# First attention of a two-layer kernel: the two heads of a pair as two 64-row tiles of TensorE

## The chip, the cores and the metric

One core of a Trainium2 chip runs the whole kernel in one launch. The metric is the device time in microseconds (us) of that core, from the first to the last instruction of the program and the little that lies around it. TensorE is called PE here, VectorE DVE, ScalarE ACT, GpSimd POOL, and SP is the queue that issues most of the DMAs. PEld is TensorE's loading of the stationary operand.

## The reference, cut to what matters

Two transformer layers over 2 x 1024 tokens of width 128, each an attention and a mixture of experts, with residuals. The change touches the first attention alone: 16 heads of width 8, softmax over 1024 keys.

```python
xn = _layernorm(x, ln_scale, ln_bias)
q = (xn @ wq).reshape(bs, sl, 16, 8).transpose(0, 2, 1, 3)   # k, v alike
scores = jnp.einsum('bhid,bhjd->bhij', q, k)
probs = jax.nn.softmax(scores / jnp.sqrt(jnp.float32(128)), axis=-1)
out = jnp.einsum('bhij,bhjd->bhid', probs, v)
out = out.transpose(0, 2, 1, 3).reshape(bs, sl, -1) + xn
```

The other stages (first mixture of 8 experts, second attention with 8 heads of width 128, second mixture of 16 experts) are the same in both kernels.

## The kernel before, in words

`layer0_project` normalises, projects to q, k and v, splits q and k into three bf16 parts each and sends the parts to DRAM. From there `load_pair` brings the rows of one pair of heads into SBUF (12 DMAs on SP): `q_stack` holds for each of the two heads (x = 0, 1) 48 rows, the products of the parts with one another (3 + 2 + 1 times 8 rows), so 96 rows for both heads, and there are two `k_stack`s, one for each head, in which the rows of the other head are zero. A product over 96 rows so gives the scores of one head. Rows 96 to 99 of `q_stack` take the negated row maxima, as a high and a low bf16 part for each head, and the same rows of `k_stack` hold ones for its own head (POOL writes them, L398). Four such stacks are in turn.

There are 16 pairs (8 of each batch). Each pair goes through two passes:

- The search: 16 tiles, each 128 queries of one head by all 1024 keys. PE makes a tile with two matmuls of 512 columns over 96 rows into one of two `max_bank`s (L504), DVE reduces it to 128 maxima (L414). After the 16 tiles PE turns the maxima (`turn_maxima`, L512), DVE splits them into two bf16 rows (`split`, L422 and L424), and SP writes them into `q_stack` (`subtract`, L367).
- The scores and their use: eight steps k, each for 128 keys. In a step PE makes four products of 512 columns over 100 rows (two heads, two halves of the queries, L537) into two `score_bank`s in turn, ACT takes the exponential of each (L483), and PE multiplies the four results of the step before with the values (`use`, L548: four 32-column tiles of the array side by side, in fp32, each shown as two records). After eight steps ACT copies the sums (`take`, L474), PE turns them (`turn_heads`, L522) and DVE divides (`divide`).

The search runs `MAX_LEAD` = 22 tiles ahead of the scores; a prologue makes those 22 tiles alone, and then each step k carries two search tiles, of the next pair or the one after it. PE's order in a step is fixed: score 0, score 1, `use` of the step before, in k = 2 `turn_heads`, in k = 6 `turn_maxima`, score 2, score 3, and the two search tiles. The waits: score e needs the exponential e - 2 to be done (its bank), `use` needs all four of its step, search tile m needs the reduction of m - 2. Score 0 of a pair waits for the DMA of the maxima (`shift_in`). All of it is a sequence written out by hand with semaphores.

At the start of the attention stage POOL fills `v_tile` (L388, L391), writes the ones of the `k_stack`s (eight instructions, L398) and then adds the residual (L402, L404, L406), while DVE stages the first values (`stage`, L431) and begins the search. In `layer0_project` POOL clears rows 0 to 95 of the `k_stack`s (L199).

Of the kernel before, what the change touches and what calls it, by code (L numbers as in the profile page):

```python
# [14 lines left out]
ALU = mybir.AluOpType  # L15
# [14 lines left out]
SHIFTS = 2 * NST  # L30
# [86 lines left out]
def load_pair(sp, t, pair, stack, loaded):  # L117
# [3 lines left out]
    for x in range(2):  # L121
        head = bass.ds(pair * (2 * HD0) + x * HD0, HD0)
        first = x * NST
        for part in range(3):
# [3 lines left out]
            sp.dma_start(t.k_stack[stack][x][rows, :], k_dram[0:3 - part, head, :]).then_inc(loaded, 16)  # L128
# [5 lines left out]
def layer0_project(nc, t, d):  # L134
    ctx = ExitStack()
    with ctx:
# [23 lines left out]
        consts_in, zeros_set = sem("consts_in"), sem("zeros_set")  # L160
        NW = 8

        with nc.Block() as block:  # L163
# [7 lines left out]
            def _(sp):  # L171
# [10 lines left out]
                sp.wait_ge(zeros_set, 2 * STACKS)  # L182
# [11 lines left out]
            def _(pool):  # L194
                pool.dma_start(t.rope[:, :, :], d["rope"].rearrange("a p s -> p a s")).then_inc(consts_in, 16)

                for stack in t.k_stack:
                    for x in range(2):
                        pool.memset(stack[x][0:SHIFTS, :], 0.0).then_inc(zeros_set, 1)  # L199
                pool.wait_ge(zeros_set, 2 * STACKS)  # L200
# [97 lines left out]
def layer0_attention(nc, t):  # L298
# [9 lines left out]
    with ctx:  # L308
# [13 lines left out]
        inverse = sb("inverse", [P, 2, P // 8])  # L322
        maxima = sb("maxima", [P, 2, TILES])
# [9 lines left out]
        rows_set, residual_step = sem("rows_set"), sem("residual_step")  # L333
        score_ready, prob_ready, used = sem("score_ready"), sem("prob_ready"), sem("used")
        plain_ready, max_ready = sem("plain_ready"), sem("max_ready")
# [24 lines left out]
        with nc.Block() as block:  # L360
            @block.sync
            def _(sp):
                def subtract(stack):

                    for part in range(2):
                        row = SHIFTS + 2 * part
                        sp.dma_start(q_stack[stack][row:row + 2, :], shift[:, part, :]).then_inc(shift_in[stack], 16)  # L367
# [18 lines left out]
            def _(pool):  # L386
# [6 lines left out]
                pool.wait_ge(ones_set, 4)  # L393
                for i in range(STACKS):
                    for x in range(2):
                        own = [t.identity[SHIFTS:P, SHIFTS + 2 * part + x:SHIFTS + 2 * part + x + 1].broadcast_to([P - SHIFTS, S])
                               for part in range(2)]
                        pool.tensor_tensor(k_stack[i][x][SHIFTS:P, :], own[0], own[1], ALU.add).then_inc(rows_set, 1)  # L398

                pool.wait_ge(rows_set, 2 * STACKS)  # L400
# [8 lines left out]
            def _(dve):  # L409
                def search(g, s, away, n):  # L410
# [3 lines left out]
                    dve.reduce_max(maxima[:, (s + away) % 2, n:n + 1], max_bank[n % 2][:, :], AX_X).then_inc(max_ready, 1)  # L414
# [32 lines left out]
                for m in range(MAX_LEAD):  # L447
                    if m == TILES + 2:
                        split(0, 0)
                    search(0, 0, *divmod(m, TILES))  # L450

                def body(g, s):
                    for k in range(TB):
                        if k == TURN_AT and ahead(g, s, 1):
                            split(g, s + 1)
                        for away, n in searched_at(k):
                            if ahead(g, s, away):
                                search(g, s, away, n)
                        if k == 3 and not first(g, s):
# [1231 lines left out]
```

## Time and profile before

| what | value |
|---|---|
| median of 3 runs | 1151.48 us (1148.94 to 1153.11) |
| span of the profiled execution | 1151.0 us |
| first attention, scores and prologue | about 41 to 453 us of the span |
| PE busy over the span | 1039.5 us (90%) |
| DVE, ACT, POOL busy | 726.9, 662.0 and 298.1 us |
| mean granted clock of PE | 0.953 |

For the profiled execution only its span is given; its own device time is not listed beside it. The span lies 0.5 us under the median of the runs, so times are worked out as differences and added to the median. In the views a row of the timeline gives the start, the length, the engine, the line, the operation with its tiles and how many instructions are merged; in square brackets stands the idle time of the engine before it and what ended it.

### The profile page before, as it was taken

Reading aid. Unit: us, or ns where it says so; the run is one execution under the profiler, and the core shown is the slowest. Engines: PE = TensorE matmul, PEld = TensorE weight load, DVE = VectorE, ACT = ScalarE, POOL = GpSimd, SP = SyncE. Lnnn points to the kernel's source line nnn. Section 1 sums busy time; section 2 is a strip of 40 time slices with the busy share of each in tenths; the row PEclk is TensorE's granted clock in tenths of the full one; section 3 lists DMA queues with packets and bytes.
Section 4 is the critical chain, followed back from the end, with each engine's and each line's share of the span. In section 5 each row is a group of like instructions: output and inputs, shape, how many; then the busy total and the mean of one; then the engine's idle time right before and its main releaser. Section 6 shows DMA issues by size and latency. Waiting matters only on the chain. (4 is left out here: it accounts for less than half of the span.)

```text
span 1151.0 us, 17518 instructions
## 1 busy us (share of the span) xinstructions
PE 1039.5 (90%) x5080; PEld 515.4 (45%) x5080; DVE 726.9 (63%) x1227; ACT 662.0 (58%) x1415; POOL 298.1 (26%) x236
## 2 busy tenths in 40 slices
PE   4499999999999995886799999999999999589997
PEld 3023333333333321422356565665656565456665
DVE  5588888888888852434544454545454544668997
ACT  4047777777777775322355545555554544357887
POOL 5640000000000000000341624343342510256675
PEclk9579999999999999688899999999999999889999
DMA  5200000000000000000000000000000000000001
GB/s 173 101 1 16 21 23 16 14 14 21 21 14 14 15 1 17 9 1 14 0 1 11 0 6 9 0 0 6 9 0 0 5 1 1 11 8 17 16 18 44
DMA packets 21227, 19.22 MB, mean 17 GB/s; under 512 B 5301, under 2 KB 15517, under 8 KB 21173
## 3 DMA queue, kind: packets, MB, share of 16 engines
q1 hardware_dynamic: 19844, 14.92, 4.4%
q0 software_dynamic: 528, 2.10, 0.5%
q10 hardware_dynamic: 800, 1.57, 0.4%
q8 instruction: 22, 0.36, 0.1%
q14 instruction: 33, 0.26, 0.1%
HBM read 14.26 MB, written 4.19 MB: 16 GB/s over the span
## 5 line engine op out<-in xcount | busy, mean ns | idle before, releaser
L483 ACT ACTIVATE probs<-score_bank 128x512 f32<-128x512 f32 x512 | 277.7, 595 | 121.2 <-PE score_bank L537 119.8
L414 DVE TENSOR_REDUCE maxima<-max_bank 128x1 f32<-128x1024 f32 x256 | 301.6, 1220 | 57.0 <-PE max_bank L504 55.0
L537 PE MATMUL score_bank<-q_stack,k_stack 100*128 100x512 bf16 x512 | 164.3, 386 | 7.0 <-ACT probs L483 5.0
L1089 ACT ACTIVATE a_probs<-a_scores,a_lowest 128x896 f32<-128x896 f32 (+7 forms) x128 | 94.7, 740 | 129.7 <-DVE a_lowest L1084 129.1
L504 PE MATMUL max_bank<-k_stack,q_stack 96*128 96x512 bf16 x512 | 143.9, 401 | 17.6 <-PEq L163 12.1
L1301 PE MATMUL a_sum<-a_turned,a_v 128*128 128x512 f32 (+3 forms) x384 | 158.5, 500 | 0.7 <-ACT a_headsT L1235 0.6
L1075 PE MATMUL a_scores<-a_kT,a_qT 128*128 128x512 f32 (+3 forms) x384 | 146.4, 500 | 2.7 <-ACT a_probs L1089 2.5
L548 PE MATMUL summed<-probs,v_tile 128*32 128x512 f32 x1024 | 136.4, 605 | 1.0 <-ACT probs L483 1.0
L1084 DVE TENSOR_REDUCE a_lowest<-a_scores 128x1 f32<-128x896 f32 (+7 forms) x128 | 96.2, 756 | 58.3 <-PE a_scores L1078 58.3
L537 PEld LDWEIGHTS score_bank<-q_stack,k_stack 100*128 100x128 bf16 x512 | 44.0, 97 | 157.4 <-ACT probs L483 143.4
L1433 POOL TENSOR_TENSOR m_gated<-m_linear,m_sigm 128x512 f32<-128x512 f32 x64 | 87.6, 1370 | 48.3 <-ACT m_sigm L1528 48.0
L708 POOL MEMSET m_padded<- 128x96 f32 x1 | 0.2, 178 | 383.4 <-POOLq L360 383.4
L1292 PE MATMUL a_turn<-identity,a_probs 128*128 128x128 f32 x576 | 95.5, 275 | 4.4 <-ACT a_probs L1089 3.5
L1180 DVE COPY a_turned<-a_turn 128x512 f32<-128x512 f32 x96 | 57.4, 598 | 63.2 <-PE a_turn L1292 62.9
L1292 PEld LDWEIGHTS a_turn<-identity,a_probs 128*128 128x128 f32 x576 | 71.5, 142 | 54.6 <-issue 47.1
L504 PEld LDWEIGHTS max_bank<-k_stack,q_stack 96*128 96x128 bf16 x512 | 48.6, 99 | 90.3 <-DVE maxima L414 22.5
L1601 PEld LDWEIGHTS m_down<-m_w,m_gated 128*128 128x128 f32 x512 | 67.8, 197 | 45.3 <-issue 41.5
L1156 POOL TENSOR_TENSOR x<-x,a_part 128x512 f32<-128x512 f32 x32 | 40.6, 1269 | 176.8 <-DVE a_part L1192 176.8
L1075 PEld LDWEIGHTS a_scores<-a_kT,a_qT 128*128 128x128 f32 x384 | 64.0, 194 | 39.1 <-issue 35.7
L1601 PE MATMUL m_down<-m_w,m_gated 128*128 128x128 f32 x512 | 71.1, 284 | 11.4 <-ACT m_scaled L1548 9.7
L1137 POOL TENSOR_TENSOR a_crossed<-a_swapped,rope 128x512 f32<-128x512 f32 x44 | 55.9, 1270 | 95.3 <-ACT a_swapped L1056 95.1
L1056 ACT ACTIVATE a_swapped<-a_proj 64x512 f32<-64x512 f32 x86 | 50.8, 591 | 49.6 <-DVE a_straight L1047 47.6
(203 smaller groups left out, 1242.8 us busy)
## 6 DMA issues: line engine op xcount, KB each, us to landing
rope<-in_rope POOLq DMA_DIRECT2D x1, 2048.0 KB, 11.4
m_w<-in_L_ffn_mlp_w SPq DMA_DIRECT2D x32, 64.0 KB, 1.7
q_stack<-q_parts SPq DMA_DIRECT2D x32, 48.0 KB
k_stack<-k_parts SPq DMA_DIRECT2D x32, 48.0 KB
q_stack<-q_parts SPq DMA_DIRECT2D x32, 32.0 KB
k_stack<-k_parts SPq DMA_DIRECT2D x32, 32.0 KB
out<-x SPq DMA_DIRECT2D x4, 256.0 KB, 2.5
q_parts<-l_q_parts SPq DMA_DIRECT2D x1, 768.0 KB, 3.5
```

Source lines behind the costliest of these rows:

```text
L414: dve.reduce_max(maxima[:, (s + away) % 2, n:n + 1], max_bank[n % 2][:, :], AX_X).then_inc(max_ready, 1)
L483: act.activation(probs[:, k % PROB_STEPS, j, :], score_bank[j % 2][:, :], ACT.Exp, scale=SCALE0).then_inc(prob_ready, 1)
L504: last = pe.matmul(max_bank[n % 2][:, half * CH:(half + 1) * CH], q_stack[stack][0:SHIFTS, qt * P:(qt + 1) * P], k_stack[stack][x][0:SHIFT ...
L537: pe.matmul(score_bank[j % 2][:, :], k_stack[s % STACKS][x][rows, k * P:(k + 1) * P], q_stack[s % STACKS][rows, half * CH:(half + 1) * CH] ...
L548: last = pe.matmul(summed[VW * j:VW * (j + 1), :], v_tile[s % 2][:, j // 2, k, :], probs[:, k % PROB_STEPS, j, :], start=(k == 0), stop=(k ...
L1075: pe.matmul(scores[n % 2][:, first:first + cols], qT[:, b, q, tile * P:(tile + 1) * P], kT[:, b, first:first + cols], start=True, stop=fir ...
L1084: dve.tensor_reduce(out=lowest[:, n % 8:n % 8 + 1], in_=scores[n % 2][:, 0:row_width(n)], op=ALU.max, axis=AX_X, negate=True).then_inc(low ...
L1089: act.activation(probs[:, k % 2, c, 0:row_width(n)], scores[n % 2][:, 0:row_width(n)], ACT.Exp, bias=lowest[:, n % 8:n % 8 + 1], accum_out ...
L1292: last_turn = pe.transpose(turn_bank[m % 2][:, c * P:(c + 1) * P], probs[:, k % 2, c, j * P:(j + 1) * P], t.identity[:, :])
L1301: pe.matmul(sum_bank[:, skipped(k, j):CH], v[:, BLOCKS[k][0], j, :], turned[:, m % SLOTS, skipped(k, j):CH], start=(j == 0), stop=(TURNED_ ...
L1433: pool.tensor_tensor(gated[:, n % 4, :], linear[:, n % 4, :], sigm[:, n % 4, :], ALU.mult).then_inc(gated_ready, 1)
L1601: last = pe.matmul(down_bank[n % 2][:, k, :], gated[:, n % 4, k * P:(k + 1) * P], w2[par][:, :], start=True, stop=True)
```

## The change

The two heads of a pair get 64 rows each. Head 0 has rows 0 to 47 and head 1 rows 64 to 111, in `q_stack` and in a single `k_stack`, so no rows of zeros are needed. Rows 48 and 49 (112 and 113) take the maxima, and POOL fills rows 32 to 63 and 96 to 127 of the `k_stack`s with ones in `layer0_project`, before the rows are loaded, so that the eight instructions of L398 are gone. Each product runs over 48 or 50 rows in the array's upper or lower half (`tile_position=(x * ROW, 0)`), and products of the two heads follow one another: scores in the order (half 0: head 0, head 1), (half 1: head 0, head 1), and a search tile is 128 queries of both heads by 512 keys, one head in each bank of `max_bank`. DVE's reduction then gives two maxima per row, one for each head, over half of the keys. A new small instruction, `join`, takes the greater of the two halves for all 16 columns, once for each pair, and `turn_maxima` waits for it. It stands behind the first search tile of step k = 5, and in the prologue behind tile 16.

```diff
-                pool.wait_ge(ones_set, 4)
-                for i in range(STACKS):
-                    for x in range(2):
-                        own = [t.identity[SHIFTS:P, ...].broadcast_to([P - SHIFTS, S]) for part in range(2)]
-                        pool.tensor_tensor(k_stack[i][x][SHIFTS:P, :], own[0], own[1], ALU.add).then_inc(rows_set, 1)
...
-                    dve.reduce_max(maxima[:, (s + away) % 2, n:n + 1], max_bank[n % 2][:, :], AX_X).then_inc(max_ready, 1)
+                    qt, half = divmod(n, 2)
+                    dve.reduce_max(halves[:, (s + away) % 2, half, :].rearrange("p (x t) -> p x t", x=2)[:, :, qt],
+                                   max_bank[n % 2][:, :].rearrange("p (x k) -> p x k", x=2), AX_X).then_inc(max_ready, 1)
+                def join(g, s):
+                    dve.wait_ge(max_ready, g * (4 * TILES) + (s + 1) * TILES)
+                    if not first(g, s):
+                        dve.wait_ge(maxT_ready, g * 4 + s)
+                    dve.tensor_tensor(maxima[:, s % 2, :], halves[:, s % 2, 0, :], halves[:, s % 2, 1, :], ALU.max).then_inc(joined, 1)
...
-                    for half in range(2):
-                        last = pe.matmul(max_bank[n % 2][:, half * CH:(half + 1) * CH], q_stack[stack][0:SHIFTS, qt * P:(qt + 1) * P],
-                                         k_stack[stack][x][0:SHIFTS, half * CH:(half + 1) * CH], start=True, stop=True)
+                    for x in range(2):
+                        rows = slice(x * ROW, x * ROW + NST)
+                        last = pe.matmul(max_bank[n % 2][:, x * CH:(x + 1) * CH], q_stack[stack][rows, qt * P:(qt + 1) * P],
+                                         k_stack[stack][rows, half * CH:(half + 1) * CH], start=True, stop=True,
+                                         tile_position=(x * ROW, 0))
...
-                    pe.wait_ge(max_ready, g * (4 * TILES) + (s + 1) * TILES)
+                    pe.wait_ge(joined, g * 4 + (s + 1))
...
-                    x, half = divmod(j, 2)
-                    rows, e = slice(0, SHIFTS + 4), s * 32 + 4 * k + j
+                    half, x = divmod(j, 2)
+                    rows, e = slice(x * ROW, x * ROW + NST + 2), s * 32 + 4 * k + j
...
-                    pe.matmul(score_bank[j % 2][:, :], k_stack[s % STACKS][x][rows, k * P:(k + 1) * P],
-                              q_stack[s % STACKS][rows, half * CH:(half + 1) * CH], start=True, stop=True).then_inc(score_ready, 1)
+                    pe.matmul(score_bank[j % 2][:, :], k_stack[s % STACKS][rows, k * P:(k + 1) * P],
+                              q_stack[s % STACKS][rows, half * CH:(half + 1) * CH], start=True, stop=True,
+                              tile_position=(x * ROW, 0)).then_inc(score_ready, 1)
```

The DMAs of `load_pair` and `subtract` keep their number and size and go to other rows.

## Rows read from the trace of the kernel before

**Rows 1.** Stretches: length; PE, PEld, DVE, ACT, POOL busy; granted clock; DMA; GB/s.
```profile
46.00:66.00 20.00, 17.73 (x37) 2.35 (x35) 19.90 (x20) 0.00 (x0) 19.84 (x9) 0.50 0.10 31
69.00:72.50 3.50, 3.50 (x9) 1.09 (x8) 2.85 (x3) 2.05 (x4) 1.99 (x1) 0.50 0.00 0
100.00:400.00 300.00, 299.07 (x1678) 94.91 (x1671) 250.27 (x277) 223.97 (x415) 0.00 (x0) 1.00 0.06 17
431.00:446.00 15.00, 12.14 (x68) 2.78 (x64) 0.55 (x2) 10.91 (x21) 0.00 (x0) 1.00 0.00 0
```

**Rows 2.** Timeline of one step k, with search (start, length in us).
```profile
270.94 0.60 PE L537 MATMUL score_bank<-q_stack,k_stack 100*128 100x512 bf16 x2
271.37 1.09 ACT L483 ACTIVATE probs<-score_bank 128x512 f32<-128x512 f32 x2 [0.50 <-PE score_bank L537]
...
272.02 2.36 DVE L414 TENSOR_REDUCE maxima<-max_bank 128x1 f32<-128x1024 f32 x2 [0.53 <-PE max_bank L504]
...
272.25 0.65 PE L537 MATMUL score_bank<-q_stack,k_stack 100*128 100x512 bf16 x2
272.50 0.10 PEld L537 LDWEIGHTS score_bank<-q_stack,k_stack 100*128 100x128 bf16 x1 [0.37 <-ACT probs L483]
...
272.82 1.06 PE L548 MATMUL summed<-probs,v_tile 128*32 128x512 f32 x8
273.82 0.60 PE L537 MATMUL score_bank<-q_stack,k_stack 100*128 100x512 bf16 x2
```

**Rows 3.** Groups by line (busy us, mean ns of one), 100 to 400 us.
```profile
L414 DVE TENSOR_REDUCE maxima<-max_bank 128x1 f32<-128x1024 f32 x201 | 236.8, 1220 | 47.6 <-PE max_bank L504 46.0
L483 ACT ACTIVATE probs<-score_bank 128x512 f32<-128x512 f32 x403 | 218.7, 595 | 74.4 <-PE score_bank L537 73.2
...
L504 PE MATMUL max_bank<-k_stack,q_stack 96*128 96x512 bf16 x403 | 103.6, 378 | 0.0
...
L431 DVE TENSOR_SCALAR v_tile<-values 128x64 f32 x24 | 3.4, 186 | 0.0
```

**Rows 4.** Timeline of one step of the last pair, without search.
```profile
440.86 0.61 PE L537 MATMUL score_bank<-q_stack,k_stack 100*128 100x512 bf16 x2
441.29 2.16 ACT L483 ACTIVATE probs<-score_bank 128x512 f32<-128x512 f32 x4 [0.72 <-PE score_bank L537]
...
443.74 0.11 PEld L537 LDWEIGHTS score_bank<-q_stack,k_stack 100*128 100x128 bf16 x2 [0.84 <-ACT probs L483]
```

**Rows 5.** Timeline, layer0_project: POOL's memsets and its next work, a small DVE operation.
```profile
2.18 7.22 POOL L199 MEMSET k_stack<- 96x1024 bf16 x8
12.15 0.18 DVE L218 TENSOR_TENSOR l_token_of_root<-l_first_inverse 128x16 f32<-128x16 f32 x1
...
21.65 2.27 POOL L205 TENSOR_TENSOR l_q_parts<-l_rest,l_q_parts 128x512 bf16<-128x512 f32 x2 [12.26 <-ACT l_q_parts L260]
```

**Rows 6.** Groups by line, PE, the whole span: a matmul over 24 rows.
```profile
L827 PE MATMUL m_wgt<-m_weightT,m_spread 24*128 24x512 bf16 x8 | 2.7, 382 | 1.0 <-DVE m_weightT L747 1.0
```

**Rows 7.** Timeline of PE in a step k = 6, with turn_maxima.
```profile
255.73 0.28 PE L512 MATMUL turned<-identity,maxima 128*16 128x128 f32 x1
...
255.84 0.60 PE L537 MATMUL score_bank<-q_stack,k_stack 100*128 100x512 bf16 x2
```

**Rows 8.** Timeline of DVE where the attention stage begins.
```profile
42.35 2.00 DVE L431 TENSOR_SCALAR v_tile<-values 128x64 f32<-128x64 f32 x2 [12.23 <-POOL v_tile L391]
44.27 2.35 DVE L414 TENSOR_REDUCE maxima<-max_bank 128x1 f32<-128x1024 f32 x2
```

**Rows 9.** Groups by line, POOL, 40 to 72 us.
```profile
L398 POOL TENSOR_TENSOR k_stack<-identity 32x1024 bf16<-32x1024 f32 x8 | 14.9, 1892 | 0.1
L402 POOL TENSOR_TENSOR normed<-normed,affine 128x2048 f32<-128x2048 f32 x1 | 4.5, 4496 | 0.1
```

**Rows 10.** Timeline of the prologue up to the first score.
```profile
59.66 2.17 PE L504 MATMUL max_bank<-k_stack,q_stack 96*128 96x512 bf16 x4 [0.19 <-DVE maxima L414]
...
69.16 1.06 PE L537 MATMUL score_bank<-q_stack,k_stack 100*128 100x512 bf16 x2
```

More of the change, by code:

```diff
@@ L29 @@
 NST = 6 * HD0
-SHIFTS = 2 * NST
+ROW = 64
 VW = 32
@@ L122, in load_pair @@
         head = bass.ds(pair * (2 * HD0) + x * HD0, HD0)
-        first = x * NST
+        first = x * ROW
         for part in range(3):
@@ L127, in load_pair @@
             sp.dma_start(t.q_stack[stack][rows, :], q_dram[part, head, :].unsqueeze(0).broadcast_to([3 - part, HD0, S])).then_inc(loaded, 16)
-            sp.dma_start(t.k_stack[stack][x][rows, :], k_dram[0:3 - part, head, :]).then_inc(loaded, 16)
+            sp.dma_start(t.k_stack[stack][rows, :], k_dram[0:3 - part, head, :]).then_inc(loaded, 16)
 def layer0_project(nc, t, d):
@@ L198, in _ @@
                     for x in range(2):
[L199 to L200 removed]
+                        pool.memset(stack[x * ROW + ROW // 2:(x + 1) * ROW, :], 1.0).then_inc(ones_set, 1)
+                pool.wait_ge(ones_set, 2 * STACKS)
                 for u in range(2 * NCH):
@@ L322, in layer0_attention @@
         inverse = sb("inverse", [P, 2, P // 8])
+        halves = sb("halves", [P, 2, 2, TILES])
         maxima = sb("maxima", [P, 2, TILES])
@@ L365, in subtract @@
                     for part in range(2):
-                        row = SHIFTS + 2 * part
-                        sp.dma_start(q_stack[stack][row:row + 2, :], shift[:, part, :]).then_inc(shift_in[stack], 16)
+                        sp.dma_start(q_stack[stack][NST + part:ROW + NST + part + 1:ROW, :], shift[:, part, :]).then_inc(shift_in[stack], 16)
                 for pair in range(1, 3):
@@ L450, in _ @@
                     search(0, 0, *divmod(m, TILES))
+                    if m == TILES:
+                        join(0, 0)
                 def body(g, s):
@@ L455, in body @@
                             split(g, s + 1)
-                        for away, n in searched_at(k):
+                        for i, (away, n) in enumerate(searched_at(k)):
                             if ahead(g, s, away):
                                 search(g, s, away, n)
+                            if k == TURN_AT - 1 and i == 0 and ahead(g, s, 1):
+                                join(g, s + 1)
                         if k == 3 and not first(g, s):
@@ L494, in search @@
                     m = (s + away) * TILES + n
-                    x, qt = divmod(n, TB)
+                    qt, half = divmod(n, 2)
                     stack = (s + away) % STACKS
@@ L546, in use @@
                     pe.wait_ge(prob_ready, g * (4 * 32) + (s * 32 + 4 * k + 4))
-                    for j in range(4):
-                        last = pe.matmul(summed[VW * j:VW * (j + 1), :], v_tile[s % 2][:, j // 2, k, :], probs[:, k % PROB_STEPS, j, :],
-                                         start=(k == 0), stop=(k == TB - 1), tile_position=(0, VW * j))
+                    for slot in range(4):
+                        x, half = divmod(slot, 2)
+                        last = pe.matmul(summed[VW * slot:VW * (slot + 1), :], v_tile[s % 2][:, x, k, :], probs[:, k % PROB_STEPS, 2 * half + x, :],
+                                         start=(k == 0), stop=(k == TB - 1), tile_position=(0, VW * slot))
                     last.then_inc(used, 1)
@@ L1634, in two_layers @@
             t.q_stack = [early_sb(f"q_stack{i}", [P, S], BF16) for i in range(STACKS)]
-            t.k_stack = [[early_sb(f"k_stack{i}_{x}", [P, S], BF16) for x in range(2)] for i in range(STACKS)]
+            t.k_stack = [early_sb(f"k_stack{i}", [P, S], BF16) for i in range(STACKS)]
             layer0_project(nc, t, d)
```

15 lines of the change are left out of this document (4 added, 11 removed).

## The prediction, written before the changed kernel ran

> **What bounds the kernel now.** I read the stretches first [rows 1]. In the steady part of the first attention PE is busy 299.07 of 300 us, DVE 250.27 and ACT 223.97, the granted clock is 1.00. That looks like a kernel bound by PE, and the change halves PE's time for eight of the twelve products of a step. But busy time of a matmul includes its fill, so I looked next at single steps.
>
> One step of the timeline, from score 2 to the next score 2 [rows 2]: 270.94 score 2; 271.37 the exponential of it starts (0.43 later). One exponential is 595 ns long [rows 3], the two together 1.09, so that of score 3 starts 0.49 later, at 271.86, and ends at 272.46. At 272.50 PE loads the weights of score 1 of the next step, which waited for ACT just there; its matmul starts at about 272.52 (two from 272.25 take 0.65, one is 378 ns [rows 3]). `use` starts 0.30 later, 272.82, and takes 1.00 to score 2 at 273.82. This is a ring:
>
> 0.43 (score 2 to its exponential) + 0.49 (to the next one) + 0.60 (that one's length) + 0.06 (to score 1) + 0.30 (to `use`) + 1.00 (to score 2) = 2.88 us, which is the whole step, 273.82 - 270.94. It exists because `use` needs all four exponentials, score 1 needs the last one, and score 2 stands behind `use` in PE's order. PE's own work between `use` and score 1 (scores 2 and 3, four search matmuls, score 0) just fits beside the ACT part: the wait for ACT ahead of the last weight load shows that it came last.
>
> Is the ring or PE's load the bound, when both are so near? The last pair answers: its steps have no search. The same step there goes from 440.86 to 443.74, again 2.88 us [rows 4], though four matmuls of some 0.22 (0.60 - 0.38 is the distance of two) are gone, 0.87 us of PE's time. ACT sat idle 0.72 before it, and DVE was busy 0.55 of 15 us in that stretch [rows 1]. So taking PE's search work away altogether saved nothing. The ring sets the step.
>
> **The steady steps, part by part.** The pairs free PE at four places. Scores 0 and 1: score 0 may start as soon as its exponential of the step before is done, but score 1 waits for the last one, 0.49 later; they can't be issued together, and score 1 is the one on the ring. Scores 2 and 3 may run together; exponential 3 starts 0.49 after exponential 2 in any case, more than the 0.22 that score 3 comes earlier. The search tiles (four times 0.22, now perhaps half) lie beside ACT. So of the ring's six terms none contains work that is taken away: 0 us. If the pairs did not overlap at all, PE would have the work of before and the result would be the same.
>
> DVE: the reduction reads the same 1024 columns; I take 1220 ns again [rows 3]. Two in a step take 2.36, with 0.53 idle [rows 2]; the added `join` is a 128x16 operation, 0.18 by the row of one [rows 5], once for each pair, behind the first tile of k = 5. It delays the second reduction, whose tile PE delivers some 0.4 earlier than before. `turn_maxima` waits for `join`, but stands in k = 6 behind `use`, more than a microsecond after it. What a late `join` would hold is the `split`, SP's two DMAs of the maxima and score 0 of the next pair: it would take about 0.5 us more before that reached score 1. Cost 0.
>
> The ring's unknowns: **fill.** A matmul's 0.38 is 0.21 of streaming (512 columns at 2.4 GHz) and 0.17 of fill. Does a 64-row tile fill faster? The nearest rows say no: 24 rows take 382 ns, 96 rows 378 [rows 3, 6], both in the whole array. Bounds: 0, or half of the fill, 0.08, once in the ring (score 2), times 127 steps = -10 us. I take 0. **Switch of the array's form.** From score 1 to `use` is 0.30 where streaming is 0.21, from `use` to score 2 it is 1.00 where the two passes of its tiles stream 0.85 to 0.90; some 0.10 are lost at each change between whole array and 32-column tiles. After the change it is between two 64-row tiles and four 32-column tiles. I take the same 0.10, because that is the nearest row; the bounds are 0.10 and the full fill of 0.17, so up to +0.07 x 2 x 127 = +18 us.
>
> **New switches.** Today `turn_maxima` is followed by score 2 after 0.11 [rows 7], its bare streaming (two passes of 128 columns at 2.4 GHz): both use the whole array. Afterwards the score is in another form. That happens on the ring, behind both kinds of turn: 15 times each. 30 x 0.10 = **+3.0 us** (bounds 0 and 30 x 0.17 = 5).
>
> The Trainium skill, "TensorEngine Tiling (Array Packing)", section Key Properties, says that a change of tiling mode drains TensorE; the same page's section Theoretical Speedup puts dimensions up to 64 at up to 2x. The trace agrees with the first by the 0.10; the second would halve the eight products, of which the ring holds nothing.
>
> **The prologue.** At its start DVE stages the first values with two small instructions. In the loop they take 186 ns each [rows 3]; here the two take 2.00, and the first reduction starts only at 44.27 [rows 8]. POOL's L398 runs just then, 1.892 us long [rows 9]: the second instruction waited for it. The change removes the eight L398, and the next in POOL's order is L402, 4.496 us long [rows 9]. It will start in the same place, at 42.4, and DVE will be held until 46.9: 4.5 - 1.9 = **+2.6 us**. The bounds are -1.8 (nothing holds DVE any more) and +2.6. I take the upper one, since the wait was as long as POOL's whole instruction.
>
> The Trainium skill, "SBUF — State Buffer", section Who interferes with whom, states this as a lock on a shared port for a whole instruction, and the 2.00 agrees. If DVE and POOL only shared the bandwidth, the length of POOL's next instruction would not matter, and the term would be 0 instead of +2.6.
>
> The tiles then run in a ring of their own at the low clock: reduction, search matmuls, next reduction, four matmuls each 2.17 + 0.19 idle = 2.36 for two tiles [rows 10]. With heads side by side PE's part shrinks and DVE's pace of 2.28 (two intervals of 2.36 - 1.22 = 1.14) is the bound: nine pairs of tiles x 0.07 = -0.6. `join` stands in this chain, +0.2. From `split` to score 0 nothing changes. The removed 14.9 us of POOL otherwise shorten only its own list. The start of the scores moves by **+2.2 us**.
>
> **The clock.** In the prologue the clock is 0.50 (1.2 GHz), in spite of PE being busy 17.73 of 20 us [rows 1]; it rose only after 3.5 us without a gap at the first scores [rows 1]. Afterwards the first step has gaps, since score 2 waits for an exponential and not for matmuls. I expect the clock to rise one step later. A step at 1.2 GHz would be 4.15 (the ring with `use` and each stream doubled: 2.88 + 0.85 + 0.21 + 0.21), so +1.3. Less 0.3, since in the first step score 2 comes 0.67 + 0.60 + 0.06 = 1.33 after score 0, by its exponential, and no longer behind four streams of 0.43: **+1.0 us**. That it holds afterwards is shown by the last pair: clock 1.00 through 431 to 446 us with PE busy 12.14 of 15 us [rows 1], and the changed steps leave PE at about the same load.
>
> **Edits at no cost.** The memsets in `layer0_project` are of ones and 32 rows instead of 96, of the same length in the free direction: 7.22 us for eight, then 12.26 idle [rows 5]. The cover would hold even at twice the length. DMAs keep number and size; SP's order is untouched. `take` stays on the ring of k = 0 as it is.
>
> **Sum.** 0 (steady) + 3.0 + 2.2 + 1.0 = +6.2 us on 1151.5: **1157.7 us**. What a measurement of this kernel can tell from no change is about 0.3%, 3.5 us.
>
> **The rivals.**
> - Ring shorter by the fill: -10 + 6 = -4, 1147 us. For it: half the rows to cross. Against: [rows 3, 6]. Chance 0.09, with 0.02 more for half of it, which is no measurable change.
> - PE is the bound after all: then the next limit is DVE, 250.27 us [rows 1] for 201 / 16 = 12.6 pairs [rows 3], 19.9 a pair and with `join` and waits some 20.6, instead of 300 / 12.6 = 23.8; 3.2 x 15 = -48, + 6: about 1110 us. Against it is the step of 2.88 without search. This is the other side in full: it decides if the steps fall below 2.8. Chance 0.05.
> - Dear switches: each costs the full fill. +18 + 2 + 6: 1178 us. A new form may drain more than a known one. Chance 0.11.
> - The low clock stays: the prologue shows 0.50 under a load that is high. Each step then costs 1.27 more, all 127 of them +161: up to 1320 us; a pair or two of them +10 to 20. For: the first line of [rows 1]. Against: at the low clock PE's streams fill over 90% of a step. Chance 0.05.
> - The change doesn't do what it says, the halves run one after the other: the steady steps as forecast, the prologue 0.6 longer, 1158 us. Chance 0.06.
>
> Forecast 0.62, with its own range 1153 to 1163. Faster by over 0.3%: 0.09 + 0.05 = 0.14. Within 0.3% (below 1155.0): 0.20 of the forecast's 0.62 (switches free, or no hold by POOL, or an early clock), 0.02 and 0.02: 0.24. Slower: 0.62. The range for 8 in 10 reaches down towards the shorter ring and up to most of the dear switches: 1148 to 1172.
>
> **What would show it.** In the changed trace: score 2 to score 2 still 2.88 us in steps with search, ACT idle about 0.7 once in a step instead of twice, waits for ACT ahead of both score 0 and score 1; PE's search tile 0.22 long instead of 0.43; `turn_maxima` to score 2 about 0.21; DVE's two L431 together 4.6 us and the first reduction near 46.9; first score near 71.4. I am wrong if the steps get shorter than 2.8 (then PE was the bound) or longer than 3.0 (switches), or if the granted clock is under 1.00 behind 80 us.

## The result and the profile after

The changed kernel takes 1168.0 us (1165.3 to 1171.4, 4 runs), the kernel before 1150.4 in the same comparison: a ratio of 1.014, interval 1.011 to 1.017, which is 16 us slower (the medians lie 17.6 apart). The forecast was +6.2 us. The direction and most of the mechanisms were right, the size was not: one term, the clock, was 17 us instead of 1 in the profiled run, which is the longest of the four (1171.4 us).

The stretches of the changed kernel come first, in the columns of [rows 1]: the first steps, the steady part, the part before the search ends, the part after it.

```profile
76.00:90.00 14.00, 14.00 (x60) 2.34 (x54) 7.07 (x6) 6.51 (x12) 0.00 (x0) 0.50 0.00 0
100.00:400.00 300.00, 262.19 (x1663) 62.15 (x1663) 249.29 (x287) 222.77 (x414) 0.00 (x0) 1.00 0.06 18
405.00:432.00 27.00, 23.16 (x148) 5.43 (x144) 20.29 (x24) 19.95 (x37) 0.00 (x0) 1.00 0.01 2
437.00:465.00 28.00, 23.90 (x86) 3.94 (x86) 0.55 (x2) 14.14 (x27) 0.00 (x0) 0.50 0.00 0
```

In the 300 us of the steady part PE has 37 us less to do than before, and DVE and ACT did nearly as much as before (249.29 for 250.27 us, 222.77 for 223.97): the pace is almost unchanged. PE's gain became idle time. The first and the last line show what changed the total: the granted clock is 0.50 at both ends of the attention. In [rows 1] it was 1.00 in the last steps, and before the change it had risen at 73 us.

One steady step of the changed kernel in its timeline, against [rows 2]:

```profile
254.95 0.39 PE L540 MATMUL score_bank<-q_stack,k_stack 50*128 50x512 bf16 x2
...
255.37 2.24 ACT L488 ACTIVATE probs<-score_bank 128x512 f32<-128x512 f32 x4 [0.72 <-PE score_bank L540]
255.60 2.35 DVE L407 TENSOR_REDUCE halves<-max_bank 128x2 f32<-128x1024 f32 x2 [0.52 <-PE max_bank L510]
...
256.02 0.87 PE L540 MATMUL score_bank<-q_stack,k_stack 50*128 50x512 bf16 x2 [0.25 <-ACT probs L488]
256.51 0.09 PEld L540 LDWEIGHTS score_bank<-q_stack,k_stack 50*128 50x128 bf16 x1 [0.40 <-ACT probs L488]
...
256.83 1.07 PE L553 MATMUL summed<-probs,v_tile 128*32 128x512 f32 x8
257.82 0.10 PEld L540 LDWEIGHTS score_bank<-q_stack,k_stack 50*128 50x128 bf16 x2 [0.84 <-ACT probs L488]
```

Two scores side by side take 0.39 together, instead of 0.60, so the tiles do overlap. And the step, from the weight load of score 2 (254.94, with the first row shown) to the next one, is 257.82 - 254.94 = 2.88 us, to the hundredth that of before. Scores 0 and 1 stand half a microsecond apart (0.87 for the two), each behind its own exponential.

The start of the attention stage, the rows that answer to [rows 8] and [rows 9], and the turn of the maxima, to [rows 7]:

```profile
43.08 4.49 POOL L394 TENSOR_TENSOR normed<-normed,affine 128x2048 f32<-128x2048 f32 x1
43.17 4.55 DVE L432 TENSOR_SCALAR v_tile<-values 128x64 f32<-128x64 f32 x2 [12.13 <-POOL v_tile L391]
...
47.64 3.47 DVE L407 TENSOR_REDUCE halves<-max_bank 128x2 f32<-128x1024 f32 x3
...
263.58 0.28 PE L519 MATMUL turned<-identity,maxima 128*16 128x128 f32 x1
...
263.79 0.39 PE L540 MATMUL score_bank<-q_stack,k_stack 50*128 50x512 bf16 x2
```

DVE's two small instructions end with POOL's long one, as forecast (4.55 us, forecast 4.6), and the turn is 0.21 ahead of the score instead of 0.11.

Where the time went can be read from the starts of `use` in both timelines. Before, the same four uses (behind the first step, four steps later, in the k = 6 of the last but one pair, the last one):

```profile
73.19 1.06 PE L548 MATMUL summed<-probs,v_tile 128*32 128x512 f32 x8
...
84.73 1.06 PE L548 MATMUL summed<-probs,v_tile 128*32 128x512 f32 x8
...
421.77 1.06 PE L548 MATMUL summed<-probs,v_tile 128*32 128x512 f32 x8
...
451.08 1.06 PE L548 MATMUL summed<-probs,v_tile 128*32 128x512 f32 x8 [0.96 <-ACT probs L483]
```

After:

```profile
75.03 1.93 PE L553 MATMUL summed<-probs,v_tile 128*32 128x512 f32 x8
...
91.57 1.06 PE L553 MATMUL summed<-probs,v_tile 128*32 128x512 f32 x8
...
430.73 1.06 PE L553 MATMUL summed<-probs,v_tile 128*32 128x512 f32 x8
...
470.86 1.94 PE L553 MATMUL summed<-probs,v_tile 128*32 128x512 f32 x8 [1.17 <-ACT probs L488]
```

The distance grows from 1.84 us to 6.84, 8.96 and 19.78. The first score comes 2.2 later (71.39 instead of 69.16; forecast 2.2). Then 0.4 is gained in the first step (forecast 0.3). Four steps at the low clock give 5.0. The 337 us in between, with 28 of the 30 turns, give 2.1. The last steps, eight of them at the low clock, give 10.8, and the last use and turn after them 1.3 more. The sum is 21.1 us at the end of the attention; the later stages, whose code is the same, gave 2.6 of it back, and the spans differ by 18.5. These stages are no fixed sum: from the start of the last `use` to the end of the span they took 699.9 us before and 697.1 to 703.9 in the profiles of the runs below that leave them and `use` as they are.

### The profile page after: what moved, and what is told of

It is laid out like the page before. It is cut to its first block and busy times, and to the rows that moved or that the text cites. A ratio compares the mean times of both kernels' runs of the same rounds, so it can differ in the third digit from the quotient of the medians.

```text
span 1169.5 us, 17540 instructions
## 1 busy us (share of the span) xinstructions
PE 1005.8 (86%) x5080; PEld 478.9 (41%) x5080; DVE 730.7 (62%) x1243; ACT 661.9 (57%) x1415; POOL 284.1 (24%) x228
## 5 line engine op out<-in xcount | busy, mean ns | idle before, releaser
L407 DVE TENSOR_REDUCE halves<-max_bank 128x2 f32<-128x1024 f32 x256 | 301.9, 1219 | 59.6 <-PE max_bank L510 59.5
L540 PE MATMUL score_bank<-q_stack,k_stack 50*128 50x512 bf16 x512 | 155.9, 409 | 49.6 <-ACT probs L488 37.9
L553 PE MATMUL summed<-probs,v_tile 128*32 128x512 f32 x1024 | 147.7, 651 | 1.2 <-ACT probs L488 1.2
L540 PEld LDWEIGHTS score_bank<-q_stack,k_stack 50*128 50x128 bf16 x512 | 36.3, 93 | 246.7 <-ACT probs L488 221.2
L510 PE MATMUL max_bank<-k_stack,q_stack 48*128 48x512 bf16 x512 | 86.0, 405 | 27.6 <-DVE halves L407 15.5
L1606 PE MATMUL m_down<-m_w,m_gated 128*128 128x128 f32 x512 | 71.4, 284 | 11.5 <-ACT m_scaled L1553 10.3
L1553 ACT ACTIVATE m_scaled<-m_down,m_column 128x128 f32<-128x128 f32 x256 | 72.0, 369 | 0.3 <-PE m_down L1606 0.3
```

What stands on the lines that cost most here:

```text
L407: dve.reduce_max(halves[:, (s + away) % 2, half, :].rearrange("p (x t) -> p x t", x=2)[:, :, qt], max_bank[n % 2][:, :].rearrange("p (x k) ...
L540: pe.matmul(score_bank[j % 2][:, :], k_stack[s % STACKS][rows, k * P:(k + 1) * P], q_stack[s % STACKS][rows, half * CH:(half + 1) * CH], s ...
L553: last = pe.matmul(summed[VW * slot:VW * (slot + 1), :], v_tile[s % 2][:, x, k, :], probs[:, k % PROB_STEPS, 2 * half + x, :], start=(k == ...
L1553: last = act.activation(scaled[:, n % 2, k, :], down_bank[n % 2][:, k, :], ACT.Copy, scale=column[n // NCH][:, tile, :])
L1606: last = pe.matmul(down_bank[n % 2][:, k, :], gated[:, n % 4, k * P:(k + 1) * P], w2[par][:, :], start=True, stop=True)
```

## The experiments

They start from the changed kernel, unless the text says that it is the kernel before.

**Extra matmuls in the steps without search.** Where the search has ended, PE makes four matmuls (`TAIL_FILL` = 4) of 48 rows by 512 columns into the free `max_bank`s, which nobody reads.

```diff
                         for tile in tiles:
                             search(g, s, *tile)
+                        if not tiles:
+                            if k == TURN_AT - 1:
+                                pe.wait_ge(max_ready, NPAIR * TILES)
+                            fill(s % STACKS, TAIL_FILL)
```

> The changed kernel, and in the eleven steps without search tiles PE makes four extra matmuls of 512 columns over 48 rows, whose results nobody reads (extra work, the output is unaffected). Theory A (the clock falls because the search ends and the paired products leave PE gaps): the granted clock stays 1.00 to the end of the attention; in the changed kernel's trace the last use started 10.8 us later against the kernel before than the use at 430.7 us did, so the time falls by 10 to 12 us. Rival B (the fall comes from the 64-row form itself, whatever the gaps): the clock still falls near 436 us and the time is the same within 1 us. Rival C (the fall is no cause, steps of 4.18 us come from a dearer switch): no change or slower by four matmuls a step.

Measured 1156.9 us (1.0052, 1.0035 to 1.0068 of before). The clock holds to the end of the attention:

```profile
437.00:458.00 21.00, 20.12 (x122) 5.37 (x114) 0.55 (x2) 14.51 (x27) 0.00 (x0) 1.00 0.00 1
```

From the `use` in the k = 6 of the last but one pair to the last one it is 29.46 us (427.66 to 457.12) instead of 40.13: 10.7 us are the clock in the last steps, and more work on PE takes them away. B and C are out. That leaves open whether idle time or thin work let the clock fall. The 11 us between the medians are not this alone: in this profile the first steps had one low step and not four, though their code is the same.

**Scores not paired.** The old order of the four scores, in which neighbours use the same 64 rows.

```diff
-                    half, x = divmod(j, 2)
+                    x, half = divmod(j, 2)
...
-  probs[:, k % PROB_STEPS, 2 * half + x, :]
+  probs[:, k % PROB_STEPS, 2 * x + half, :]
```

> The changed kernel with the scores in the old order (head 0 half 0, head 0 half 1, head 1 half 0, head 1 half 1), so that scores 0 and 1, and 2 and 3, use the same 64 rows and can't overlap; the search stays paired. Theory A (gaps in time on PE decide the clock): each step has 0.22 us more of streaming, as much in the last steps as the kernel before had there, and before the clock held; so the clock holds through the last pair, at the start it rises some steps earlier, and the time falls by 10 to 15 us. Rival B (the number of rows in use counts, not only the time): 50 rows for as long as 100 before are half the rows, so the clock falls at 436 us again, same time. In both, steady steps stay 2.88 us, since the ring does not hold the overlap.

Measured 1166.7 us (1.0143, 1.0103 to 1.0184): no gain. The clock in the last steps:

```profile
428.00:446.00 18.00, 14.33 (x81) 3.22 (x77) 1.31 (x6) 13.20 (x26) 0.00 (x0) 1.00 0.01 2
449.00:462.00 13.00, 11.73 (x42) 1.47 (x42) 0.00 (x0) 6.03 (x12) 0.00 (x0) 0.50 0.00 0
```

PE now streams in these steps for as long as in the kernel before, where the clock held for all of them ([rows 1]: busy 12.14 of 15, here 14.33 of 18). It held to 447 us instead of 436 and then fell all the same. The later moment says little: with the paired scores and the same last steps it fell at 440 and at 454 us in two of the runs below. But the fall itself, at as much streaming as before, does not fit my theory A, gaps in time, and rows at work became the better one.

**POOL waits for the staged values.** One line, `pool.wait_ge(staged, 2)`, ahead of the residual work.

> The changed kernel, but POOL begins its residual work only when DVE has staged the first values. Theory: the two staging instructions take about 0.3 us instead of 4.55, the first reduction starts 4.3 us earlier and the first score too, so -4.3 us, if the clock rises the same number of steps later. Rival: POOL's work held nothing, the 4.55 has another cause (the first touch of the tile, the loading of values): no change. Third: the residual work now ends later but is finished long before it is read, so it costs nothing either way.

Measured 1157.8 us (1.0050, 1.0034 to 1.0067), 10 us less than the changed kernel instead of 4.3.

```profile
43.38 0.30 DVE L433 TENSOR_SCALAR v_tile<-values 128x64 f32<-128x64 f32 x2 [12.19 <-POOL v_tile L391]
```

The two instructions take 0.30. The first score comes at 67.3 instead of 71.4, the forecast 4; and the clock rose at 75 us, one step after the first use, so that three of the four low first steps were gone too (3.9 us). At the end, where the code is that of the changed kernel, the clock fell at 440 us, and four steps were low instead of eight (5.5 us). Why an earlier start also shortens the time at the low clock I can't tell.

**The same in the kernel before**, where the first of POOL's instructions is shorter (`pool.wait_ge(staged, 2)` in place of the wait ahead of L398).

> The kernel before, and POOL writes the ones of the k_stacks only when DVE has staged the first values. Theory of the shared port: the 2.00 us of the two staging instructions become 0.3, the first reduction comes 1.7 us earlier, so does the first score (POOL's ones are ready long before), and the time is 1.7 us less, 0.15%. Rival: POOL's late ones now hold something (score 0 waits for them): 0 or slower.

Measured 1150.7 us, ratio 0.9978 (0.9960 to 0.9995): 2.5 us less, with 1.7 expected inside the interval. The two instructions took 0.30, the first score came at 67.5.

**Extra matmuls at the first scores**, of 48 rows and of 128 rows:

```diff
                     search(0, 0, *divmod(m, TILES))
+                    warm({TILES + 3: 3, TILES + 4: 2}.get(m, 0))
...
                         if first(g, s) and k == 0:
+                            warm(1)
```

> The changed kernel with six extra matmuls of 512 columns over 48 rows ahead of and in the first step of the scores (three behind search tile 19, two behind tile 20, one between score 1 and the first search tile), results unused. Theory A (PE had gaps in the first steps and in the wait for the maxima, and these keep the clock low): the clock rises near 73 us instead of 91, four steps of 4.18 us become 2.88, -5 us, less up to 0.5 for the matmuls that stand in the way. Rival B (rows count): the extra work is as narrow as the rest, so the clock rises at about the same step, 0 to +0.5 us.

> As the run with six extra matmuls of 48 rows at the first scores (it had 1166.6 us, clock up at 92 us in its profile), but each of the six goes over all 128 rows, results unused. Theory R (rows at work count, which the kernel before with 50-row scores showed over the whole attention): the clock rises near 73 to 76 us and the time is 3 to 6 us less, about 1162. Rival (only time counts): the same number of matmuls of the same length, so again 1166 to 1167.

Measured 1166.6 us (1.0132, 1.0115 to 1.0149) and 1168.7 us (1.0110, 1.0077 to 1.0144). Neither helped: the clock rose at 92 and at 88 us in the profiles, and the first score came 0.8 and 1.2 us later than in the changed kernel. In the wide run single runs went from 1161 to 1171. Six matmuls, wide or narrow, did not decide it, and the forecast of both theories for the wide ones failed.

The wide run's profile shows something else. Its last steps are those of the changed kernel, yet the clock held to 454 us, and two steps were low instead of eight:

```profile
437.00:453.00 16.00, 11.85 (x72) 2.69 (x72) 0.55 (x2) 12.01 (x23) 0.00 (x0) 1.00 0.00 0
```

Its last `use` starts at 463.04, 7.8 us earlier than in the changed kernel, and the span is only 2.6 shorter: the later stages took the rest. So the loss in the last steps is not a fixed 10.8 us for this code. In the four profiles with the same last steps it was 10.8, 10.8, 5.4 and 2.8.

The changed kernel itself has two groups of runs, 1165.3 with a mean clock of 0.943 and 1171 with 0.930. Four low steps more or less would be 4 x 1.3 = 5.2 us, but only a run of the longer group was traced, so it is not shown that this is the difference. The unpaired run, with the same two mean clocks, was traced in its shorter group: there both ends were better, with the clock up at 79 us and down at 447.

**Scores over 50 rows in the kernel before, and over 96 as its control.** The first is a pure test of the rows: no tiles, no pairs, the old order. Both leave out the subtraction of the maxima, the first the second head's rows too.

```diff
-                    rows, e = slice(0, SHIFTS + 4), s * 32 + 4 * k + j
+                    rows, e = slice(0, 50), s * 32 + 4 * k + j        # control: slice(0, SHIFTS)
```

> The kernel before (whole array, one head for each product, nothing paired), but each score product runs over rows 0 to 49 of the stacks instead of 0 to 99: it leaves out the rows of the second head and the subtraction of the maxima. Same instructions, same streaming time, half the rows at work in the scores. Theory R (the rows that are at work count for the granted clock): the clock falls in the last steps as it did in the changed kernel with unpaired scores (447 us there), and the time grows by 5 to 9 us. Theory T (the form of the tiles or the time alone counts): the clock holds to the end of the attention as before, time the same within 2 us.

> Control for the run in which the kernel before had scores over 50 rows (1206 us, low clock to 267 us in its profile): the same kernel with scores over rows 0 to 95. It too leaves out the subtraction of the maxima, so that probabilities are larger, but both heads' rows are at work. Theory R (rows at work count): the clock rises at 73 us and holds, time as before within 3 us. Rival D (the other data, larger probabilities and sums in use, kept the clock low there): a low clock here too and 1190 us or more.

Over 50 rows: 1206 us, ratio 1.041 (1.036 to 1.045). Its profile is of its longest run, 1269 us, with a mean clock of 0.866; the four that the ratio rests on took 1195 to 1207, with 0.919 to 0.933, against 0.950 to 0.954 of the kernel before. Taken as means over time between 0.50 and 1.00, these give an estimate of 50 to 90 us more at the low clock than in the kernel before, and of 230 for the profiled run. So the direction holds for every run, the 150 us below for the longest alone. In the profile the clock stays low until 267 us. Over 96 rows: 1152.5 us, 0.9991 (0.9971 to 1.0011), clock up at 73 us. The stretch from 100 to 250 us, 50 rows and then 96 (in the second fence):

```profile
100.00:250.00 150.00, 150.00 (x433) 25.61 (x432) 65.46 (x72) 57.64 (x107) 0.00 (x0) 0.50 0.03 10
```

```profile
100.00:250.00 150.00, 149.52 (x843) 47.55 (x835) 124.67 (x137) 111.98 (x208) 0.00 (x0) 1.00 0.06 17
```

PE is busy without a gap for 150 us and the clock stays at 1.2 GHz: how long PE is busy does not decide the clock alone. But low it is only until it has once risen. From 268 to 537 us the same products run at the full clock:

```profile
350.00:400.00 50.00, 50.00 (x267) 13.46 (x266) 39.73 (x45) 35.49 (x67) 0.00 (x0) 1.00 0.05 16
```

What bears on the changed kernel's main loss is the end, the eleven steps without search. Over 50 rows, ahead of the fall and behind it:

```profile
531.00:537.00 6.00, 4.67 (x25) 0.90 (x24) 0.37 (x3) 4.87 (x10) 0.00 (x0) 1.00 0.01 3
540.00:560.00 20.00, 18.69 (x60) 3.11 (x56) 0.55 (x2) 9.77 (x18) 0.00 (x0) 0.50 0.00 0
```

Over 96 rows, at about the same steps:

```profile
428.00:434.00 6.00, 4.66 (x28) 0.92 (x24) 0.00 (x0) 4.93 (x10) 0.00 (x0) 1.00 0.00 0
434.00:450.00 16.00, 13.14 (x74) 2.90 (x66) 0.55 (x2) 11.20 (x22) 0.00 (x0) 1.00 0.00 0
```

PE is busy 4.67 and 4.66 of 6 us. With 50 rows the clock then falls and the steps become 4.18 us, as in the changed kernel; with 96 it holds to the end. No tile, pair or order of scores differs between the two, so it is the rows of the score products that let the clock fall. The missing subtraction is in both, so it is not the cause. One difference in the data is not separated: over 50 rows the second head's products keep two of its own rows. The changed kernel and its unpaired version, whose products are whole, lose the clock at the same end.

**Both repairs together.**

> The changed kernel with both repairs: extra matmuls in the eleven steps without search, and POOL's residual work only when DVE has staged the first values. If the two causes are separate they add up: -11 us and -9 us as measured one by one against the changed kernel's 1168, of which the second held some of the start's low clock too; 1150 to 1154 us. If they are one cause seen twice (the later part of the clock's fall moved), 1156.

Measured 1155.9 us (1.0017, 1.0000 to 1.0033). That is the 1156 forecast for one cause seen twice. In the profiles of both runs with one repair three of the four low first steps were already gone, so that part of their gains is the same one. And the later stages took part of the gain: the last `use` starts at 452.32, 4.8 us earlier than with the extra matmuls alone, the span is 1.8 shorter. What is left against the kernel before is 2 us. In the profile the turns cost 2.3 and the one low step 1.1, and 2.3 are gained ahead of them and in the first step.

**The ring opened: `use` in two parts.** The claim under the whole prediction is that the step is a ring of waits through `use`. If so, it must get shorter when only half of `use` stands in it. Both repairs are in these kernels, other than in the kernel before with the same cut.

```diff
-                def use(g, s, k):
+                def use(g, s, k, part):
+                    cols = slice(part * (CH // 2), (part + 1) * (CH // 2))
...
+                        if done:
+                            use(*done, 0)      # behind score 1
...
                         for j in range(2, 4):
                             score(g, s, k, j)
+                        if done:
+                            use(*done, 1)      # behind score 3
                         for tile in tiles:
                             search(g, s, *tile)
```

> The kernel with both repairs, and the use of the probabilities cut into two parts of 256 columns, one behind score 1 and one behind score 3; ACT takes the heads behind the fourth exponential of k = 0. Theory (a ring of waits through use sets the step at 2.88 us): from score 1 to score 2 only half of use remains, about 0.84 us instead of 1.30; then PE's order and DVE (2.28 for two reductions and 0.25 of other work a step) are the limit, a step of 2.5 to 2.6, so 127 x 0.3 = 38 us less, 1112 to 1120 us. Rival (DVE or the banks set the step already): no gain, and slower by two more changes of the array's form in each step, 127 x 0.2 = +25 us.

Measured 1160.6 us (1.0079, 1.0047 to 1.0111), not 1115. Its timeline shows a second ring:

```profile
252.19 0.38 PE L548 MATMUL score_bank<-q_stack,k_stack 50*128 50x512 bf16 x2
...
252.68 2.16 ACT L490 ACTIVATE probs<-score_bank 128x512 f32<-128x512 f32 x4 [0.80 <-PE score_bank L548]
...
253.34 0.87 PE L548 MATMUL score_bank<-q_stack,k_stack 50*128 50x512 bf16 x2 [0.19 <-ACT probs L490]
...
254.14 0.64 PE L562 MATMUL summed<-probs,v_tile 128*32 128x256 f32 x8
...
254.71 0.61 PE L512 MATMUL max_bank<-k_stack,q_stack 48*128 48x512 bf16 x4
...
255.15 0.38 PE L548 MATMUL score_bank<-q_stack,k_stack 50*128 50x512 bf16 x2
```

Scores 0 and 1 now stand together at 252.19; score 3 waits for exponential 1 (253.82), then the second part of `use` (254.14), then the search (254.71), then score 0 again: 2.96 us, of which the search is 0.44.

That is not all of the time. Twice, where PE goes back to the start of its loop over the pairs, it stands idle for about 3 us and waits for nothing that the trace shows, and the clock falls with it (for 10.2 us from 190.6 on, for 6.8 from 289.6 on):

```profile
189.55 0.51 PE L548 MATMUL score_bank<-q_stack,k_stack 50*128 50x512 bf16 x2 [3.00 <-issue]
...
290.76 0.72 PE L548 MATMUL score_bank<-q_stack,k_stack 50*128 50x512 bf16 x2 [2.93 <-issue]
```

No run with `use` in one piece has such a gap there. The cut doubles the matmuls of `use`, and the queue that brings instructions moved twice as much, here and in the three runs below; first without the cut (both repairs), then with it:

```profile
q8 instruction: 22, 0.36, 0.1%
...
q8 instruction: 44, 0.72, 0.2%
```

So the longer loop is probably fetched anew on each pass; no run tests this. Away from the gaps a pair of eight steps mostly takes 23.5 to 23.9 us instead of 24.02 uncut: a step with a turn is no longer than the others. The four pairs at the gaps take 26.8, 27.1, 26.9 and 24.9. These 11 us turn a gain of 5 into a loss.

**The kernel before with the same cut.**

> The kernel before, whole array, with the same cut of use. Theory: the ring is opened here too, but now PE's own work is the limit: 12 streams of 0.22, 0.87 of them search, use 0.85, four changes of form at 0.1, together about 3.0 us, so the step gets no shorter than 2.9 to 3.05 and the time is 1150 to 1172 us. If the gain of the cut is as large here as in the kernel with two 64-row tiles, the pairing has no part in it.

Measured 1204.5 us (1.0448, 1.0425 to 1.0471), outside of what I expected. The step is 3.40 us:

```profile
249.97 0.64 PE L549 MATMUL summed<-probs,v_tile 128*32 128x256 f32 x8
...
253.37 0.64 PE L549 MATMUL summed<-probs,v_tile 128*32 128x256 f32 x8
```

That is the second ring with the search of before in it: 2.96 - 0.44 + 0.87 = 3.39. My sum of PE's work missed it. The two gaps are here too (2.36 and 2.50 us), with 3.4 us of low clock behind each. The pairing matters here as it never did in the closed ring: the search costs half.

**The search between score 1 and score 2**, and then **one search tile in each ring**:

> The run with use cut in two had steps of 2.96 us: score 0 to its exponential 0.49, this and the next 0.49 + 0.60, score 3 0.07 later, 0.32 to the second part of use, 0.57, and then the search 0.44 ahead of the next score 0: a new ring through the search. Here the search tiles stand behind the first part of use, where PE waited for an exponential. Theory: the ring loses the 0.44, steps of 2.5 to 2.6 us, with DVE nearly as long; 127 x 0.35 = 44 us less than the 1160 of that run, about 1115, less what a low clock gives back. Rival (something else holds the steps, DVE's reductions or ACT): no shorter than 2.9.

Measured 1173.2 us (1.0161, 1.0139 to 1.0183), worse than the first cut, although the step is no longer. In its profile the clock rose at 91.6 us instead of 74.6, which costs 6 us in the first pair, a pair takes 24.1 us, since the turns stand in the ring again, and the two gaps and the low clock behind them cost 11. The first parts of `use`:

```profile
256.48 0.64 PE L562 MATMUL summed<-probs,v_tile 128*32 128x256 f32 x8
257.05 0.61 PE L512 MATMUL max_bank<-k_stack,q_stack 48*128 48x512 bf16 x4
...
259.36 0.64 PE L562 MATMUL summed<-probs,v_tile 128*32 128x256 f32 x8
```

2.88 us again: the search's 0.44 moved into the first ring (last exponential, score 1, first part of `use`, score 2), which without it would be 2.45. The two together tell what each ring can bear.

> Two rings were measured with use cut in two: last exponential, score 1, first part of use, score 2, exponentials 2 and 3: 2.89 us with the search's 0.44 in it (2.45 without); and score 0, exponentials 0 and 1, score 3, second part of use, score 0: 2.96 with the 0.44 in it (2.52 without). Here one search tile stands in each, 0.22: 2.67 and 2.74, so the step is 2.74 us, 127 x 0.22 = 28 us less than the 1160.6 of the first of the two, 1133, and 15 more or less by the clock. Rival (the rows of these two runs misread, another limit near 2.9): 1155 to 1175.

```profile
265.27 0.64 PE L562 MATMUL summed<-probs,v_tile 128*32 128x256 f32 x8
265.84 0.39 PE L512 MATMUL max_bank<-k_stack,q_stack 48*128 48x512 bf16 x2
...
266.53 0.64 PE L562 MATMUL summed<-probs,v_tile 128*32 128x256 f32 x8
267.10 0.39 PE L512 MATMUL max_bank<-k_stack,q_stack 48*128 48x512 bf16 x2
...
267.94 0.64 PE L562 MATMUL summed<-probs,v_tile 128*32 128x256 f32 x8
```

The step shown is 267.94 - 265.27 = 2.67 us; a pair with its turns takes 22.2 to 22.7, 2.8 a step. The time is 1140.1 us, ratio 0.9887 (0.9862 to 0.9912): the first version that beats the kernel before, by 13 us. The expected 1133 was too low by 7. The gaps account for that: PE is idle for 2.63 and 2.67 us at the loop's return, the clock falls for 3 us near 184 and for 10 near 276, and the four pairs there take 9 us more than the others.

```profile
275.66 0.72 PE L548 MATMUL score_bank<-q_stack,k_stack 50*128 50x512 bf16 x2 [2.67 <-issue]
```

## Why the prediction was right and wrong

- **The ring sets the step, 0 us from the pairs.** Right. The step stayed 2.88 us although PE lost 37 of 300 us of busy time, and the ring gave way only when `use` was cut: a pair of eight steps went from 24.02 us to 22.2 to 22.7 with one search tile in each ring.
- **Fill and switches.** Right in kind: score 2 to its exponential is 0.43 as before, `use` to score 2 1.00. The new switch behind a turn is 0.10. The 337 us between the outer uses hold 28 of the 30 turns and grew by 2.1 us where 2.8 were forecast for them, 0.08 each.
- **The prologue, +2.2.** Right to the tenth at the first score; within it the hold by POOL was 2.55 (forecast 2.6), the tiles' pace and `join` gave back 1.14 (forecast 0.4), and the stage itself began 0.82 later, for which I have no cause.
- **The clock, +1.0. This is the step that failed.** In the profiled run it measured 5.0 us in the first steps, 10.8 in the last ones and 1.3 behind them, 17.1, less the 0.4 gained in the first step: 16.7. The price of a low step was right, 4.18 us for a forecast 4.15 (79.21 - 75.03, by the starts of `use` there). The expectation that the clock rises one step later failed by three steps. What failed above all was the sentence that the last pair shows that the clock holds, since "the changed steps leave PE at about the same load". Load was read as busy time, and even that was less: PE is busy 11.85 of 16 us in such steps at the full clock (in the run with wide extra matmuls), and was 12.14 of 15. And the row had scores over 100 rows; the changed ones go over 50. Unpaired scores brought the busy time back, and the clock still fell; over 50 rows it fell and over 96 it held, with nothing else changed in the kernel before. As a rival ("The low clock stays") I had it at 0.05, "a pair or two" of low steps at +10 to 20, and for a reason in time only. The size of the term is partly luck of the run: in the four profiles with these last steps the loss there was 2.8 to 10.8 us.
- **The rival of the dear switches** would have given 1178 us and is not what happened, although its time is near: the switches cost 0.08 to 0.10.
- **Open.** What sets the moment at which the clock rises in the first steps: with the same code there it was 91 us in the profile of the changed kernel and 79 in that of the run with extra matmuls at the end, and extra matmuls ahead of it did nothing. What sets the moment of the fall: 436, 437, 440 and 454 us with the same last steps. Why the later stages, with the same code, took 697 to 704 us. Why PE stands idle at the loop's return with `use` cut.

## What to carry to other kernels

When the busiest engine is relieved, look first for a stretch of the same trace in which its work is already missing: here the last pair's steps, as long without search as with it, showed that PE's load did not set the pace. A relieved TensorE may also lose its clock, and busy time alone does not tell: here scores over half of the rows lost it where those over nearly all of them, at the same busy time, did not. So compare the rows at work too. The room that such a change makes is worth something only when the ring of waits is opened for it, and where the freed work then stands decides which ring it lengthens. A cut that doubles the instructions in a loop has a price of its own: look for gaps at the loop's return.

## What the runs showed of the hardware that was not expected

- PE busy for 150 of 150 us, with scores over 50 rows beside products over 96 and 128, at a granted clock of 0.50 (in the longest run of that kernel); with scores over 96 rows and the same instructions the clock was 1.00. Once risen, it was 1.00 with 50 rows too, for 270 us, until the search ended.
- PE idle for 2.4 to 3.4 us at the loop's return in the four kernels with `use` cut, with 0.72 MB on the instruction queue instead of 0.36, and in no other.
- Two matmuls of 512 columns in two 64-row tiles take 0.39 us together, where one takes 0.38: the overlap is nearly complete.
- A matmul over 50 rows in a 64-row tile has the same fill as one over 100 in the whole array (0.43 from score to exponential in both).
- DVE's two instructions, 0.30 us together when POOL waits, took 4.55 us beside a POOL instruction of 4.49. The Trainium skill, "SBUF — State Buffer", section Who interferes with whom, speaks of a lock for a whole instruction, and this row and the 0.30 without it agree.
